# Layer 2 of a graph network: the edges' source product in float32r parts instead of float32

## The chip, the cores and the metric

The kernel runs on one core of one Trainium2 chip. The metric is the device time of one execution in microseconds (us). TensorE (PE) multiplies, ScalarE (ACT) and VectorE (DVE) read PSUM and SBUF, GpSimd (POOL) issues the indirect transfers, SyncE (SP) issues most of the others.

## The reference

There are 100,000 nodes with 128 features and 25,000 weighted edges, sorted by destination. Cut to what matters here:

```
h = relu(layernorm(x));  xn = bn0(h)
h1 = bn1(relu(gcn(xn) @ W1 ...))            # 128 -> 256
h2 = bn2(relu(agg(h1) @ Wrel2 + brel2 + h1 @ Wroot2))   # 256 -> 256
h3 = bn3(relu(agg(h2) @ Wrel3 + brel3 + h2 @ Wroot3))   # 256 -> 128
agg(h)[d] = sum over edges e into d of ew[e] * h[src[e]]
out = x + h3
```

`_bn` normalizes over the nodes and `_gcn_conv` is a weighted sum over the edges plus a self term, multiplied by W1.

## The kernel before

A node without an incoming edge needs only a dense product, and a destination of an edge needs more. So each layer has a dense part (98 tiles of 1024 nodes) and an edge part (49 chunks of 512 edges, 128 channels on the partitions, 512 edges along the free axis). Both are interleaved on every engine. The phases are: setup, norm (layernorm, and a fold of the first norm into W1), layers l1, l2, l3, and out.

Each engine has one in-order stream that `pipeline` writes out: in each turn the stages of `edge_layer`, then those of `dense_layer`, then `edges_ahead`; a chunk has a turn every second dense tile. A stage has a lag: the turn it runs in, counted in chunks. In layer 2 the lags are 1 for turning the gathered rows and making z (`l_turn`), 2 for the product of z (`l_src`), 3 for the weighted running sums (`l_sum`), 4 for their product with Wrel2 (`l_rel`), 5 for the destinations (`l_dst`). A PE stage waits on semaphores, and nothing behind it on the engine can pass it.

For the source end of an edge layer 2 makes its input again: `source_z` (VectorE, L1380 and L1383) multiplies the loaded rows `ed_hs` by the inverse degree and adds the turned gathered sum, which gives z; `source` (PE, L1298) multiplies z by W1 in two blocks of 128 columns; `source_relu` (ScalarE, L1466) evicts them; `affine` and `sums` go on from there. The other products of layer 2 are made in parts: a value is cast to float32r (top), the difference is kept (rest), and top*w_top + rest*w_top + top*w_rest are added up in PSUM. That is how the dense tiles (casts L1130, rests L1162, products L1103, evictions L1117), the sums (`sum_top` L1511, `sum_rest` L1421, `rel` L1314) and the destinations (L1534, L1524, `dst` L1338) are multiplied. The product of z is in plain float32.

The order of the edge stages on ScalarE and VectorE, as the kernel writes it (each with its lag), and the wait ahead of the product of z:

```
stages = [(l_rel, sum_top), (l_dst, table_out(0))] if n < 3 else []      # scalar
stages += [(l_dst, dst_relu)]
stages += [(l_dst, table_out(1))] if n == 2 else []
stages += [(l_src, source_relu), (l_src, affine)]

stages = [(l_rel, sum_rest)] if n == 2 else []                           # vector
stages += [(l_dst, statistics)]
stages += [(l_turn, source_z)] if n == 2 else []
stages += [(l_sum, sums)]

wait_use(pe, zz[j], i, 2)                                                # source
```

`table_out` (L1490) evicts the rows that `table` (PE, L1352) turned, `dst_relu` (L1502) evicts the destinations' product, and `statistics` (L1409) takes its moments. `turn` (PE, L1277) turns the gathered rows.

Of the kernel before, what the change touches and what calls it, by code (L numbers as in the profile page):

```python
# [23 lines left out]
FP = mybir.dt.float32  # L24
FR = mybir.dt.float32r
BF = mybir.dt.bfloat16
I32 = mybir.dt.int32
# [6 lines left out]
C = 128  # L34
# [72 lines left out]
def wait_use(eng, sem, i, per=1, upto=None, base=0):  # L107


    if isinstance(i, int) and i < 0:  # L110
        return
    eng.wait_ge(sem, i * per + (base + (per if upto is None else upto)))
# [83 lines left out]
def before(i, j, d, slots):  # L196

    return i - (d - j + slots - 1) // slots if d > j else i, (j - d) % slots
# [12 lines left out]
def build(nc, x, src, dst, ew, prm, out):  # L211
# [47 lines left out]
    with keep:  # L259
        def sb(name, shape, dt=FP):  # L260
            return keep.enter_context(nc.sbuf_tensor(name, shape, dt))
# [16 lines left out]
        out_c = sb("out_cols", [P, ET], I32)  # L278
        ew_c = sb("weight_cols", [P, ET])
        rounds_first = sb("rounds_first", [1, 2, EI], I32)  # L280
        rounds_norm = sb("rounds_norm", [1, 3, EI], I32)
        zeros_c = sb("zeros_c", [128, 1])
        no_edge_row = sb("no_edge_row", [P, 1, 1])
        neg_share = sb("neg_share_of_dst", [128, 1])
# [6 lines left out]
        def middle_sb(name, shape, dt=FP):  # L291
            return middle.enter_context(nc.sbuf_tensor(name, shape, dt))

        w1, wrel[2] = middle_sb("w1", [C, 1, H1]), middle_sb("wrel2", [C, 2, H1])
        wparts[2], wrel_parts = [[middle_sb(f"{name}_{part}", [C, 2, H1], FR) for part in ("top", "rest")] for name in ("wroot2", "wrel2")]
        dst_c, inv_c = middle_sb("dst_cols", [P, ET], I32), middle_sb("inv_deg_src_cols", [P, ET])
        front = middle.enter_context(ExitStack())
# [1 line left out]
        def front_sb(name, shape, dt=FP):  # L299
            return front.enter_context(nc.sbuf_tensor(name, shape, dt))  # L300

        wroot[2], wfold[1] = front_sb("wroot2", [C, 2, H1]), front_sb("w1_fold", [C, 1, H1])
        moments = front_sb("moments0", [C, TC])
        mval = front_sb("map_values", [P, ET, 2])
        src_c = front_sb("src_cols", [P, ET], I32)

# [863 lines left out]
        def edge_layer(ph, n, ps, slots):  # L1170
# [45 lines left out]
            for j in range(slots):  # L1216
                stood[j] += 16 * EG * uses(slots, j)
            if n == 2:
                inv = ph.sb("ed_inv", [C, slots, CW])
                s_top, s_rest, d_top = (ph.sb(f"ed_{x}", [C, kb, CW], FR) for x in ("sum_top", "sum_rest", "hd_top"))  # L1220
                d_rest = hd_in.bitcast(FR)
                s_tp, s_rs, d_tp, d_rs = (ph.slots(f"ed_{x}", slots) for x in ("sum_top", "sum_rest", "hd_top", "hd_rest"))
                ag = ph.sb("ed_rel", [C, slots, 2, CW])
                tb = ph.sb("ed_rows", [P, slots, EG, kb * C])
                tiles = tab[n][0:EP, :].rearrange("(t p g) c -> t p g c", p=P, g=EG)
                halves = kb
                hg = EG // halves
# [42 lines left out]
            def tensor(pe):  # L1270
# [9 lines left out]
                def source(i, j):  # L1280
                    i1, j1 = before(i, j, 1, slots)
                    if n == 2:
                        wait_use(pe, zz[j], i, 2)
                    else:
                        wait_use(pe, in_a[j], i, 16)
                        wait_use(pe, gat[j], i, 16 * EG, base=base[j])
                    for m in range(2):
                        wait_use(pe, rl_s[j1], i1, 2, m + 1)
                        o = ps[:, BS + m, 0:CW]
                        if n == 3:  # L1290

                            for g in range(EG):
                                ins = pe.matmul(ps[:, BS + m, g * P:(g + 1) * P], tg[:, j, g, m * C:(m + 1) * C], ident[0:P, 0:P],
                                                start=g == 0, stop=False, is_transpose=True, skip_group_check=True)
                            ins.then_inc(tu[j], 1)
                        for k in range(ks):
                            w = w1 if n == 2 else wfold[2]
                            ins = pe.matmul(o, w[:, k, m * C:(m + 1) * C], hsi[:, j, k, :],  # L1298
                                            start=n == 2 and k == 0, stop=k == ks - 1, skip_group_check=n == 3)
                        ins.then_inc(mm_s[j], 1)  # L1300

                def products(parts, top, rest, k, m):
# [70 lines left out]
            def vector(dve):  # L1373
                dve.memset(zero[:, :], 0.0).then_inc(z0, 1)
                dve.wait_ge(z0, 1)

                def source_z(i, j):

                    wait_use(dve, in_a[j], i, 32)
                    dve.tensor_tensor(hsi[:, j, 0, :], hsi[:, j, 0, :], inv[:, j, :], ALU.mult).then_inc(zz[j], 1)  # L1380
                    wait_use(dve, zz[j], i, 2, 1)
                    wait_use(dve, tu[j], i)
                    dve.tensor_tensor(hsi[:, j, 0, :], hsi[:, j, 0, :], ps[:, BG, 0:CW], ALU.add).then_inc(zz[j], 1)  # L1383

                def sums(i, j):
                    wait_use(dve, in_b[j], i, 16 * (4 - n))
                    if n == 3:
                        wait_use(dve, spr[j], i)
                    for k in range(kb):
                        wait_use(dve, aff[j], i, kb, k + 1)  # L1390
                        weight = cf[:, j, :] if n == 2 else ps[:, BW[j], 0:CW]
                        dve.tensor_tensor(xa[:, j, k, :], xa[:, j, k, :], weight, ALU.mult).then_inc(msg[j], 1)

                    if n == 2:
                        wait_use(dve, mm_r[j], i - 1, mb)
                    else:
                        wait_use(dve, mm_d[j], i - 1, mb)
                    i1, j1 = before(i, j, 1, slots)
                    wait_use(dve, scn[j1], i1, kb)
                    for k in range(kb):  # L1400
                        wait_use(dve, msg[j], i, kb, k + 1)
                        fresh = isinstance(i1, int) and i1 < 0
                        start = zero[:, 0:1] if fresh else se[:, j1, k, CW - 1:CW]
                        dve.tensor_tensor_scan(se[:, j, k, :], ss[:, j, :], xa[:, j, k, :], start, ALU.mult, ALU.add).then_inc(scn[j], 1)
                def statistics(i, j):
                    for m in range(mb):
                        wait_use(dve, rl_d[j], i, mb, m + 1)
                        dve.sem_inc(gate_d, 1)
                        dve.bn_stats(stats[:, m, NT * CH + i * slots + j, :], dst_out(i, j, m)).then_inc(st_d[j], 1)  # L1409

                def weights(i, j):
                    wait_use(dve, spr[j], i - 1)
                    dve.sem_inc(gate_w, 1)
                    dve.tensor_copy(cw[:, j, :], ew_c[:, bass.ds((i * slots + j) * EG, EG)]).then_inc(cwc[j], 1)

                def sum_rest(i, j):
                    i1, j1 = before(i, j, 1, slots)
                    wait_use(dve, mm_r[j1], i1, mb)
                    for k in range(kb):
                        wait_use(dve, s_tp[j], i, kb, k + 1)  # L1420
                        dve.tensor_tensor(s_rest[:, k, :], se[:, j, k, :], s_top[:, k, :].bitcast(FP), ALU.subtract).then_inc(s_rs[j], 1)  # L1421

                stages = [(l_rel, sum_rest)] if n == 2 else []
                stages += [(l_dst, statistics)]
                stages += [(0, weights)] if n == 3 else []
                stages += [(l_turn, source_z)] if n == 2 else []
                stages += [(l_sum, sums)]

                def end():
                    for j in range(slots):  # L1430
                        dve.wait_ge(st_d[j], mb * uses(slots, j))

                return slots, stages, end

            def scalar(act):
# [74 lines left out]
                        wait_use(act, scn[j], i, kb, k + 1)  # L1510
                        act.activation(s_top[:, k, :], se[:, j, k, :], ACT.Copy).then_inc(s_tp[j], 1)  # L1511

                stages = [(l_rel, sum_top), (l_dst, table_out(0))] if n < 3 else []
                stages += [(l_dst, dst_relu)]
                stages += [(l_dst, table_out(1))] if n == 2 else []
                stages += [(l_src, source_relu), (l_src, affine)]
# [25 lines left out]
        def fold(ph, n, blocks, groups, weight, folded, b_in, b_out, ps=None):  # L1542
# [25 lines left out]
            def vector(dve):  # L1568
                done = [0]

                def link(ins):
                    done[0] += 1
                    ins.then_inc(s, 1)
                    dve.wait_ge(s, done[0])
# [44 lines left out]
                if n in (1, 2):  # L1619
                    for (w_top, w_rest), w in ((wparts[n + 1], folded), (wrel_parts, wrel[2]))[:3 - n]:  # L1620
                        link(dve.tensor_copy(w_top[:, :, :], w[:, :, :]))
                        link(dve.tensor_tensor(w_rest[:, :, :], w[:, :, :], w_top[:, :, :].bitcast(FP), ALU.subtract))
                for m in range(b_in.shape[1]):
                    dve.wait_ge(pd, m + 1)
                    link(dve.tensor_tensor(b_out[:, m:m + 1], b_in[:, m:m + 1], ps[:, m, 0:1], ALU.add))
# [183 lines left out]
```

## Time and profile before

| | |
|---|---|
| median of 3 runs | 3447.38 us (3444.28 to 3447.8) |
| the profiled execution | 3449.69 us, its span 3447.9 us |
| busy in the span | PE 2844.8, DVE 2603.7, ACT 2310.8, POOL 1310.1 us |
| layer 2 | from about 1119 to 2205 us of the span |

The span runs from the first to the last instruction. Matmuls overlap, so the start of one to the start of the next tells more than the duration of one; their ends are modelled. A float32 matmul has two records. "f32" in the type of a matmul stands for float32 and float32r alike. In brackets is the idle time of the engine just before an instruction and what ended it. In a table of windows the columns are: the stretch, its length, busy time (and instructions) of PE, of the weight loads PEld, of DVE, ACT and POOL, then the granted clock of TensorE as a share of 2.4 GHz, the busy share of the DMA engines, and GB/s.

### The profile page before, as it was taken

Reading aid. Unit: us, or ns where it says so; the run is one execution under the profiler, and the core shown is the slowest. Engines: PE = TensorE matmul, PEld = TensorE weight load, DVE = VectorE, ACT = ScalarE, POOL = GpSimd, SP = SyncE. Lnnn points to the kernel's source line nnn. Section 1 sums busy time; section 2 is a strip of 40 time slices with the busy share of each in tenths; the row PEclk is TensorE's granted clock in tenths of the full one; section 3 lists DMA queues with packets and bytes.
Section 4 is the critical chain, followed back from the end, with each engine's and each line's share of the span. In section 5 each row is a group of like instructions: output and inputs, shape, how many; then the busy total and the mean of one; then the engine's idle time right before and its main releaser. Section 6 shows DMA issues by size and latency. Waiting matters only on the chain. (4 is left out here: it accounts for less than half of the span.)

```text
span 3447.9 us, 51737 instructions
## 1 busy us (share of the span) xinstructions
PE 2844.8 (83%) x12445; PEld 1955.9 (57%) x12445; DVE 2603.7 (76%) x5601; ACT 2310.8 (67%) x4070; POOL 1310.1 (38%) x1196
## 2 busy tenths in 40 slices
PE   3666499999997899999999999699999999554542
PEld 2666355555554677777777777555555555443432
DVE  6999388888888788888888888678888888533332
ACT  4999377777775688888888887466666667333331
POOL 1657656556551421111211110132222221266576
PEclk9999799999998999999999999899999999655555
DMA  5999499999996799999999999589999998799997
GB/s 193 344 344 328 133 333 345 339 342 340 337 339 253 271 345 344 346 347 344 344 347 346 344 348 329 185 295 339 340 339 341 340 339 316 288 365 363 381 357 227
DMA packets 335138, 1106.81 MB, mean 321 GB/s; under 512 B 54569, under 2 KB 102210, under 8 KB 285906
## 3 DMA queue, kind: packets, MB, share of 16 engines
q1 hardware_dynamic: 211964, 905.05, 71.8%
q0 software_dynamic: 62656, 77.70, 10.0%
q10 hardware_dynamic: 60438, 123.18, 9.9%
q8 instruction: 27, 0.44, 0.1%
q14 instruction: 53, 0.43, 0.0%
HBM read 599.13 MB, written 498.21 MB: 318 GB/s over the span
## 5 line engine op out<-in xcount | busy, mean ns | idle before, releaser
L1265 POOL DMA_INDIRECT l_ed_gathered<-agg_rows,pos_cols x392 | 399.8, 1020 | 1419.1 <-PE l_ps L1277 699.8
L1162 DVE TENSOR_TENSOR dense_tiles<-dense_tiles,l_dn_top 128x512 fp32r<-128x512 f32 x784 | 501.7, 688 | 235.1 <-ACT l_dn_top L1130 235.1
L1103 PE MATMUL l_ps<-l_dn_top,wroot_top 128*128 128x512 f32 x1176 | 502.6, 427 | 73.2 <-ACT l_dn_ho L1117 43.3
L1130 ACT ACTIVATE l_dn_top<-dense_tiles 128x512 fp32r<-128x512 f32 x784 | 447.8, 623 | 32.1 <-issue 31.7
L1103 PE MATMUL l_ps<-l_dn_top,wroot_rest 128*128 128x512 f32 x1176 | 468.3, 398 | 0.0
L1103 PE MATMUL l_ps<-dense_tiles,wroot_top 128*128 128x512 f32 x1176 | 463.0, 394 | 0.0
L745 PE MATMUL l_ps<-l_dn_columns,w_fold 128*128 128x512 f32 x784 | 382.0, 610 | 31.0 <-ACT l_dn_ho L780 31.0
L1117 ACT ACTIVATE l_dn_ho<-l_ps,bias_fold 128x512 f32<-128x512 f32 x392 | 263.4, 685 | 160.0 <-PE l_ps L1103 159.5
L1733 PE MATMUL out_ps<-ident,dense_tiles 128*128 128x128 f32 x784 | 185.6, 415 | 208.6 <-ACT dense_tiles L1720 208.6
L1103 PEld LDWEIGHTS l_ps<-l_dn_top,wroot_top 128*128 128x128 f32 x1176 | 222.6, 189 | 183.3 <-ACT l_dn_ho L1117 64.2
L1749 DVE TENSOR_TENSOR out_od_ot<-out_ps,x_tiles 128x512 f32<-128x512 f32 x196 | 134.7, 691 | 246.9 <-PE out_ps L1733 242.8
L627 ACT ACTIVATE norm_ln_ho<-norm_ln_x,norm_ln_nbias,norm_ln_rstd 128x128 f32<-128x128 f32 x784 | 301.7, 480 | 0.0
L639 PE MATMUL norm_ln_ps<-norm_ln_ho 128*128 128x130 f32 x1568 | 202.8, 282 | 116.7 <-ACT norm_ln_ho L627 116.7
L780 ACT ACTIVATE l_dn_ho<-l_ps,bias_fold 128x512 f32<-128x512 f32 x392 | 260.3, 694 | 47.7 <-PE l_ps L745 40.7
L1720 ACT ACTIVATE dense_tiles<-dense_tiles,bn_shift,bn_scale 128x1024 f32<-128x1024 f32 x98 | 121.3, 1239 | 252.0 <-DMA dense_tiles<-h_dense 242.4
L1733 PEld LDWEIGHTS out_ps<-ident,dense_tiles 128*128 128x128 f32 x784 | 148.8, 217 | 245.2 <-ACT dense_tiles L1720 161.8
L863 POOL DMA_INDIRECT l_ed_dst_rows<-h_rows,dst_cols x196 | 208.8, 1065 | 167.7 <-PE l_ps L945 117.9
L639 PEld LDWEIGHTS norm_ln_ps<-norm_ln_ho 128*128 128x128 f32 x1568 | 184.2, 191 | 135.5 <-ACT norm_ln_ho L627 135.5
L1103 PEld LDWEIGHTS l_ps<-dense_tiles,wroot_top 128*128 128x128 f32 x1176 | 223.5, 190 | 58.1 <-issue 12.0
L669 POOL DMA_INDIRECT h_rows<-map_values,out_cols x196 | 189.5, 967 | 169.6 <-issue 154.1
L1103 PEld LDWEIGHTS l_ps<-l_dn_top,wroot_rest 128*128 128x128 f32 x1176 | 222.6, 189 | 54.5
L745 PEld LDWEIGHTS l_ps<-l_dn_columns,w_fold 128*128 128x128 f32 x784 | 134.1, 191 | 208.4 <-ACT l_dn_ho L780 140.9
(247 smaller groups left out, 6245.9 us busy)
## 6 DMA issues: line engine op xcount, KB each, us to landing
h_dense<-l_dn_ho SPq DMA_DIRECT2D x188, 1024.0 KB, 10.8
dense_tiles<-h_dense SPq DMA_DIRECT2D x188, 1024.0 KB, 8.6
l_dn_rows<-h_rows SPq DMA_DIRECT2D x98, 520.0 KB, 6.9
h_rows<-norm_ln_ho SPq DMA_DIRECT2D x97, 520.0 KB, 4.3
h_dst<-l_ed_ho SPq DMA_DIRECT2D x98, 512.0 KB, 6.3
l_ed_hd<-h_dst ACTq DMA_DIRECT2D x98, 512.0 KB
norm_ln_x<-in_x SPq DMA_DIRECT2D x97, 512.0 KB, 5.4
x_tiles<-in_x SPq DMA_DIRECT2D x97, 512.0 KB, 15.3
```

The source lines that it names most:

```text
L627: ins = act.activation(ho[:, j, g, 0:C], xt[:, j, g, :], ACT.Relu, bias=nb[:, j, g:g + 1], scale=rs[:, j, g:g + 1])
L639: ins = pe.matmul(ps[:, 0, 0:TC], ho[0:rows, j, g, 0:C], ho[0:rows, j, g, :], start=first and g == 0, stop=final and g == G - 1, skip_grou ...
L669: pool.indirect_dma_start(h0[:, :], bass.IndirectOffsetOnAxis(ap=out_c[0:rows, t:t + 1], axis=0), mval[0:rows, t, :], None, element_offset ...
L745: pe.matmul(ps[:, 2 + u % 2, 0:CW], wfold[1][:, 0, m * C:(m + 1) * C], hc[:, j % 2, c * CW:(c + 1) * CW], start=True, stop=True).then_inc( ...
L780: act.activation(ho[:, j, m, c * CW:(c + 1) * CW], ps[:, 2 + u % 2, 0:CW], ACT.Relu, bias=bfold[1][:, m:m + 1]).then_inc(rl[j], 1)
L863: pool.indirect_dma_start(to[:, j, g, :], None, h0[0:N, :], bass.IndirectOffsetOnAxis(ap=idx[:, t:t + 1], axis=0)).then_inc(gat[j], 16)
L1103: ins = pe.matmul(o, a, b, start=t == 0, stop=t == len(terms) - 1)
L1117: act.activation(ho[:, j, m, c * CW:(c + 1) * CW], ps[:, u % 2, 0:CW], ACT.Relu, bias=bf[:, m:m + 1]).then_inc(rl[j], 1)
L1130: act.activation(top[:, j % 2, k, cc], hi[:, j, k, cc], ACT.Copy).then_inc(tp[j], 1)
L1162: dve.tensor_tensor(rest[:, j, k, cc], hi[:, j, k, cc], top[:, j % 2, k, cc].bitcast(FP), ALU.subtract).then_inc(spl[j], 1)
L1265: pool.indirect_dma_start(tg[:, j, g, :], None, tab[n - 1][:, :], bass.IndirectOffsetOnAxis(ap=pos_c[:, t:t + 1], axis=0)).then_inc(gat[j] ...
L1733: ins = pe.transpose(ps[0:P, bank0 + (j % 2) * banks + b, g * C:(g + 1) * C], hi[:, j, e:e + P], ident[:, :])
```

## The change

The product of z with W1 in layer 2 is made like the others, in float32r parts. W1's parts are made once, in the fold at the end of the norm phase. ScalarE casts z to `ed_z_top` in the new stage `z_cast`, VectorE makes `ed_z_rest` in the new stage `z_remainder`, both with the lag of the product, and the product waits for the remainder. Each part has one buffer. `w1` and `rounds_norm` move to memory that is given back after layer 1.

```diff
             if n == 2:
+                z_top, z_rest = ph.sb("ed_z_top", [C, CW], FR), ph.sb("ed_z_rest", [C, CW], FR)
+                z_tp, z_rs = ph.slots("ed_z_top", slots), ph.slots("ed_z_rest", slots)
...
                     if n == 2:
-                        wait_use(pe, zz[j], i, 2)
+                        wait_use(pe, z_rs[j], i)
...
-                        for k in range(ks):
-                            w = w1 if n == 2 else wfold[2]
-                            ins = pe.matmul(o, w[:, k, m * C:(m + 1) * C], hsi[:, j, k, :],
-                                            start=n == 2 and k == 0, stop=k == ks - 1, skip_group_check=n == 3)
+                        mc = slice(m * C, (m + 1) * C)
+                        if n == 2:
+                            terms = [(w1_top[:, mc], z_top[:, :]), (w1_top[:, mc], z_rest[:, :]), (w1_rest[:, mc], z_top[:, :])]
+                        else:
+                            terms = [(wfold[2][:, k, mc], hsi[:, j, k, :]) for k in range(ks)]
+                        for t, (a, b) in enumerate(terms):
+                            ins = pe.matmul(o, a, b, start=n == 2 and t == 0, stop=t == len(terms) - 1, skip_group_check=n == 3)
                         ins.then_inc(mm_s[j], 1)
...
+                def z_remainder(i, j):
+                    wait_use(dve, z_tp[j], i)
+                    dve.tensor_tensor(z_rest[:, :], hsi[:, j, 0, :], z_top[:, :].bitcast(FP), ALU.subtract).then_inc(z_rs[j], 1)
...
-                stages += [(l_turn, source_z)] if n == 2 else []
+                stages += [(l_src, z_remainder), (l_turn, source_z)] if n == 2 else []
...
-                stages = [(l_rel, sum_top), (l_dst, table_out(0))] if n < 3 else []
+                def z_cast(i, j):
+                    i1, j1 = before(i, j, 1, slots)
+                    wait_use(act, mm_s[j1], i1, 2)
+                    wait_use(act, zz[j], i, 2)
+                    act.activation(z_top[:, :], hsi[:, j, 0, :], ACT.Copy).then_inc(z_tp[j], 1)
+
+                stages = [(l_src, z_cast), (l_rel, sum_top), (l_dst, table_out(0))] if n < 3 else []
...
+                if n == 0:
+                    link(dve.tensor_copy(w1_top[:, :], w1[:, 0, :]))
+                    link(dve.tensor_tensor(w1_rest[:, :], w1[:, 0, :], w1_top[:, :].bitcast(FP), ALU.subtract))
```

On VectorE the edge turn of a steady period of layer 2 reads so before the change, from the remainders of the sums over the statistics of the destinations and z to the running sums:

```order
L1421 TENSOR_TENSOR l_ed_sum_rest<-l_ed_sum,l_ed_sum_top 128x512 x2
L1409 BN_STATS bn_stats_all<-l_ed_ho 128x6 x2
L1380 TENSOR_TENSOR l_ed_hs<-l_ed_hs,l_ed_inv 128x512
L1383 TENSOR_TENSOR l_ed_hs<-l_ed_hs,l_ps 128x512
L1392 TENSOR_TENSOR l_ed_xa<-l_ed_xa,l_ed_coef 128x512 x2
L1404 SCALAR_TENSOR_TENSOR l_ed_sum<-l_ed_same,l_ed_sum,l_ed_xa 128x512 x2
```

And so with the change, in which the line numbers are higher by up to 19:

```order
L1431 TENSOR_TENSOR l_ed_sum_rest<-l_ed_sum,l_ed_sum_top 128x512 x2
L1419 BN_STATS bn_stats_all<-l_ed_ho 128x6 x2
L1393 TENSOR_TENSOR l_ed_z_rest<-l_ed_hs,l_ed_z_top 128x512
L1386 TENSOR_TENSOR l_ed_hs<-l_ed_hs,l_ed_inv 128x512
L1389 TENSOR_TENSOR l_ed_hs<-l_ed_hs,l_ps 128x512
L1402 TENSOR_TENSOR l_ed_xa<-l_ed_xa,l_ed_coef 128x512 x2
L1414 SCALAR_TENSOR_TENSOR l_ed_sum<-l_ed_same,l_ed_sum,l_ed_xa 128x512 x2
```

The remainder of z stands behind the statistics of the destinations and ahead of the next chunk's z; nothing else moved.

On ScalarE the same place with the change is the following, from the last casts of a dense tile to the evictions of the product of z:

```order
L1131 ACTIVATE l_dn_top<-dense_tiles 128x512 x2
L112 ISA x2
L1527 ACTIVATE l_ed_z_top<-l_ed_hs 128x512
L112 ISA
L112 REGISTER_ALU
L1521 ACTIVATE l_ed_sum_top<-l_ed_sum 128x512 x2
L112 REGISTER_ALU
L1500 ACTIVATE l_ed_rows<-l_ps 128x512
L112 ISA
L1512 ACTIVATE l_ed_ho<-l_ps,bias_fold 128x512 x2
```

The row of `l_ed_z_top` is new and stands ahead of the casts of the sums; the two evictions `l_ed_ho`, for which the statistics on VectorE wait, come three stages behind it.

## Rows read from the trace of the kernel before

**Rows 1.** Windows of the steady part of layer 2 (columns as told above).

```profile
1160.00:2100.00 940.00, 898.06 (x3913) 676.54 (x3912) 810.33 (x1227) 760.28 (x1312) 181.02 (x176) 1.00 0.98 344
```

**Rows 2.** Waits in 1160 to 2100 us: us in total, times, longest.

```profile
PE l_ps L1103 <- ACT l_dn_ho L1117: 39.8, 43, 2.0
```

**Rows 3.** Timeline of PE in one period: start, us, instruction.

```profile
1610.45 0.66 PE L1352 MATMUL l_ps<-ident,l_ed_rel 128*128 128x128 f32 x4
1610.94 0.60 PE L1277 MATMUL l_ps<-ident,l_ed_gathered 128*128 128x128 f32 x4
1611.38 1.88 PE L1298 MATMUL l_ps<-l_ed_hs,w 128*128 128x512 f32 x4
...
1613.34 0.39 PE L1314 MATMUL l_ps<-l_ed_sum_rest,wrel_top 128*128 128x512 f32 x1
...
1615.67 0.40 PE L1314 MATMUL l_ps<-l_ed_sum_top,wrel_rest 128*128 128x512 f32 x1
...
1632.84 1.88 PE L1298 MATMUL l_ps<-l_ed_hs,w 128*128 128x512 f32 x4
```

**Rows 4.** Timeline of ACT in the same period.

```profile
1608.77 1.15 ACT L1511 ACTIVATE l_ed_sum_top<-l_ed_sum 128x512 fp32r<-128x512 f32 x2
1609.81 0.59 ACT L1490 ACTIVATE l_ed_rows<-l_ps 128x512 f32<-128x512 f32 x1
1610.29 0.69 ACT L1502 ACTIVATE l_ed_ho<-l_ps,bias_fold 128x512 f32<-128x512 f32 x1
...
1610.86 0.69 ACT L1502 ACTIVATE l_ed_ho<-l_ps,bias_fold 128x512 f32<-128x512 f32 x1
...
1612.44 0.69 ACT L1466 ACTIVATE l_ed_ho_src<-l_ps,bias 128x512 f32<-128x512 f32 x1 [0.30 <-PE l_ps L1298]
```

**Rows 5.** Timeline of DVE in the same period.

```profile
1609.60 1.29 DVE L1421 TENSOR_TENSOR l_ed_sum_rest<-l_ed_sum,l_ed_sum_top 128x512 fp32r<-128x512 f32 x2
1611.24 1.29 DVE L1409 BATCH_NORM_STATS2 bn_stats_all<-l_ed_ho 128x512 f32 x2 [0.35 <-ACT l_ed_ho L1502]
1612.44 0.68 DVE L1380 TENSOR_TENSOR l_ed_hs<-l_ed_hs,l_ed_inv 128x512 f32<-128x512 f32 x1
1613.15 0.69 DVE L1383 TENSOR_TENSOR l_ed_hs<-l_ed_hs,l_ps 128x512 f32<-128x512 f32 x1
...
1621.52 1.29 DVE L1162 TENSOR_TENSOR dense_tiles<-dense_tiles,l_dn_top 128x512 fp32r<-128x512 f32 x2 [1.73 <-ACT l_dn_top L1130]
```

**Rows 6.** Timelines at two waits of PE that end, with what ended one.

```profile
1164.88 1.28 DVE L1421 TENSOR_TENSOR l_ed_sum_rest<-l_ed_sum,l_ed_sum_top 128x512 fp32r<-128x512 f32 x2
...
1165.62 0.50 PE L1314 MATMUL l_ps<-l_ed_sum_top,wrel_top 128*128 128x512 f32 x1 [2.10 <-DVE l_ed_sum_rest L1421]
...
1603.84 0.50 PE L1103 MATMUL l_ps<-l_dn_top,wroot_top 128*128 128x512 f32 x1 [0.87 <-ACT l_dn_ho L1117]
1604.18 0.39 PE L1103 MATMUL l_ps<-dense_tiles,wroot_top 128*128 128x512 f32 x1
```

**Rows 7.** Timelines of PE and DVE at the first chunk of layer 2.

```profile
1143.98 1.88 PE L1298 MATMUL l_ps<-l_ed_hs,w 128*128 128x512 f32 x4
...
1145.21 1.29 DVE L1162 TENSOR_TENSOR dense_tiles<-dense_tiles,l_dn_top 128x512 fp32r<-128x512 f32 x2 [0.32 <-ACT l_dn_top L1130]
1146.42 0.69 DVE L1380 TENSOR_TENSOR l_ed_hs<-l_ed_hs,l_ed_inv 128x512 f32<-128x512 f32 x1
```

**Rows 8.** Timeline at the end of the norm phase: last fold step, a scatter.

```profile
361.41 0.17 DVE L1627 TENSOR_SCALAR quiet<-bias_fold 128x2 f32<-128x2 f32 x1
...
364.45 0.91 POOL L669 DMA_INDIRECT h_rows<-map_values,out_cols  x1 [0.30 <-issue]
```

**Rows 9.** A wait of PE, and windows with the granted clock behind two waits.

```profile
1189.39 0.50 PE L1103 MATMUL l_ps<-l_dn_top,wroot_top 128*128 128x512 f32 x1 [1.60 <-ACT l_dn_ho L1117]
...
1167.10:1170.20 3.10, 3.10 (x9) 2.33 (x9) 2.06 (x4) 0.79 (x2) 2.38 (x3) 0.50 1.04 412
...
1189.40:1192.80 3.40, 3.40 (x18) 2.82 (x18) 0.86 (x2) 2.24 (x5) 0.00 (x0) 1.00 1.01 385
```

More of the change, by code:

```diff
@@ L280, in build @@
         rounds_first = sb("rounds_first", [1, 2, EI], I32)
-        rounds_norm = sb("rounds_norm", [1, 3, EI], I32)
         zeros_c = sb("zeros_c", [128, 1])
@@ L292, in middle_sb @@
             return middle.enter_context(nc.sbuf_tensor(name, shape, dt))
-        w1, wrel[2] = middle_sb("w1", [C, 1, H1]), middle_sb("wrel2", [C, 2, H1])
+        wrel[2] = middle_sb("wrel2", [C, 2, H1])
+        w1_top, w1_rest = middle_sb("w1_top", [C, H1], FR), middle_sb("w1_rest", [C, H1], FR)
         wparts[2], wrel_parts = [[middle_sb(f"{name}_{part}", [C, 2, H1], FR) for part in ("top", "rest")] for name in ("wroot2", "wrel2")]
@@ L302, in build @@
         wroot[2], wfold[1] = front_sb("wroot2", [C, 2, H1]), front_sb("w1_fold", [C, 1, H1])
-        moments = front_sb("moments0", [C, TC])
+        w1, moments = front_sb("w1", [C, 1, H1]), front_sb("moments0", [C, TC])
+        rounds_norm = front_sb("rounds_norm", [1, 3, EI], I32)
         mval = front_sb("map_values", [P, ET, 2])
```

## The prediction

> **What bounds the kernel now.** I read the stages first (the windows by stretch), then the waits of layer 2, then one period of its loop instruction by instruction, because the change only touches the edge chunks of layer 2 and a small fold ahead of layer 1. In the steady part of layer 2 [rows 1] TensorE is busy 898.06 of 940 us at full clock, VectorE 810.33, ScalarE 760.28, and the DMA engines 98%. One period (one chunk of 512 edges and two dense tiles) is 21.45 us: the product of z starts at 1611.38 and again at 1632.84 [rows 3]. The DMA share looks like a second bound, but the waits of this stretch name no dense tile or store; what TensorE waits for is ScalarE's eviction of the dense tile's products, 39.8 us in 43 times [rows 2], 0.93 us each. So the loop runs at TensorE's pace, plus one short stop per period. What holds up TensorE once per period holds up all of layer 2. The other engines have room: VectorE idles 1.73 us before the dense rests [rows 5].
>
> What sets the place of each engine near the product of z is the order in which each one takes its stages. TensorE does the last products for the destinations, turns the second half of the table (1610.45), turns the gathered rows (1610.94) and goes straight into the product of z at 1611.38 [rows 3]. ScalarE at that moment is not ahead but behind: from 1608.77 it casts the sums' top, evicts table rows (1609.81), evicts the two destination products (1610.29 and 1610.86), back to back, and only then waits for the product of z [rows 4]. VectorE follows ScalarE: the statistics of the destinations start at 1611.24 and the next instruction at 1612.44 [rows 5]. Today the product of z doesn't care, since its z was finished a period ago.
>
> **The change part by part.** (a) *The product itself.* The two float32 products are four matmul records, and from the first to the second record of the product behind them it takes 1613.34 - 1611.38 = 1.96 us. Eleven float32r matmuls from 1613.34 to 1615.67 are 10 steps, 0.233 us each [rows 3]. So the old product takes 1.96 - 0.233 = 1.73 us, the new one 6 x 0.233 = 1.40: TensorE gains 0.33 us a chunk, 16 us over 49 chunks. If nothing waited this would be the result.
>
> (b) *The cast on ScalarE.* The new cast stands ahead of the casts of the sums. Two such casts take 1.04 us of the queue (1608.77 to 1609.81 [rows 4]), so one takes 0.52. Its inputs are long ready (z was added up in the previous period, the product before has been done for a period). But ScalarE is back to back there, so everything behind it moves by 0.52: the table eviction that the second turn of the table waits for, and the eviction of the destination products, the last of which starts at 1610.86 + 0.52 = 1611.38.
>
> (c) *The remainder on VectorE.* It stands behind the destination statistics and ahead of the next chunk's z. The statistics wait for those evictions (they start 0.26 us after the first one's end, 1610.29 + 0.69 [rows 4, 5]), so they move by the same 0.52 and VectorE is free at 1612.44 + 0.52 = 1612.96. A subtraction of this size takes 0.69 (the row of the z addition, 0.69, and two remainders in 1.29 [rows 5]): the remainder ends at 1613.65. TensorE restarts 0.05 behind such a subtraction: the first of the pair at 1164.88 ends at about 1165.57, TensorE goes on at 1165.62 [rows 6]. So the product of z can start at 1613.70 instead of 1611.38: **TensorE stands 2.32 us**. The wait is at the head of the product and holds the queue: behind it are the twelve products of the sums, then both dense tiles, and ScalarE's source evictions wait for it too. None of them can pass.
>
> (d) *Restart.* After a wait the first matmul takes 0.34 to the next one's start (1603.84 to 1604.18 [rows 6]) instead of 0.233: +0.11.
>
> Per chunk: 2.32 + 0.11 - 0.33 = **+2.10 us**. Does something take it back? The stop of 0.87 us before a dense product at 1603.84 [rows 6] comes from ScalarE's order behind TensorE's own evictions, so it moves along with TensorE and stays. ScalarE has 0.52 and VectorE 0.69 more work in a period that grows by 2.1; neither becomes the bound. The gathers wait for the turn, which moves only 0.5. Transfers get more time.
>
> How many chunks: 46 of 49 have the destination stages in the loop (they start 3 chunks later than the products of z): 46 x 2.10 = 96.6 us. For the first three, VectorE stands in the dense rests instead: the product is at 1143.98, the last rests start at 1145.21 and the next instruction, whose place the remainder takes, at 1146.42, so the remainder ends at 1147.11, TensorE goes on at 1147.16, a stop of 3.18; with (a) and (d) +2.96 each, 9 us [rows 7].
>
> (e) *The fold of the first norm* gets two more VectorE instructions on half of 128x512, each below 0.69 [rows 5], say 0.6 together. I take it at nothing: VectorE's last step of the fold is at 361.41 while GpSimd still issues scatters at 364.45 [rows 8], and the stage ends for all engines together. Uncovered it would cost 0.6. The moved buffers cost nothing in time; I find no stage that uses another amount of memory traffic.
>
> (f) *The clock.* Layer 2 has had some longer stops of TensorE. After the one of 2.10 us at 1165.62 [rows 6] the granted clock was 0.50 (1.2 GHz) from 1167.1 to 1170.2, with 9 matmuls in 3.1 us; after the one of 1.60 at 1189.39 it stayed at 1.00 (2.4 GHz) with 18 in 3.4 us [rows 9]. At 0.233 a matmul, 3.1 us would hold 13.3, so such a stretch loses 4.3 x 0.233 = 1.0 us by the count and up to half of 3.1, 1.55, by the level of the clock. I take 1.5. The new stop of 2.32 is cut in two by the turns: 0.52 before the second turn of the table, 1.8 before the product. That lies between the two cases seen. I choose one fall in nine chunks, 5 x 1.5 = 7.5 us; the ends are none and all 49 (73 us).
>
> The Trainium skill ("TensorE: Matmul & The Clock Gate", section "HAM oscillation — how this bites in real kernels") says that a loop whose waits let the clock fall pays for it again in each iteration. By that rule, if it applies here, the time is the upper end, 3626 us; the trace has both cases, a fall after 2.10 and none after 1.60, so it bears the rule out only for the longer stops.
>
> **Sum.** 96.6 + 9 + 7.5 = 113 us on the profiled execution's 3449.7 us (span 3447.9) gives 3562.8; the runs' median 3447.4 is 2.3 lower, so **3560 us**.
>
> **The rivals.**
> 1. *The clock falls often.* The same stop, but the half clock comes in every second chunk or more: 3447.4 + 105.6 + 25 to 49 times 1.5 = 3590 to 3626. For it: a fall after 2.10. Against it: the turns break the stop, and none fell after 1.60.
> 2. *The stop is shorter.* If ScalarE's cast finds room (0.52 drops out), a chunk costs 1.58: 46 x 1.58 + 9 = 82, 3529. Against it: ScalarE shows no idle time from 1608.77 to the eviction at 1610.86, and the table's turn waits for it already.
> 3. *Faster: the remainder is ready in time.* Then only (a) is left, 3447.4 - 16 = 3431. It decides at one point: the subtraction would have to end by 1611.33. VectorE's statistics alone, ahead of it, don't end before 1612.44 today. It needs VectorE to run the remainder ahead of the statistics, which the order doesn't do. The same with a stop of just 0.2 a chunk is no change.
> 4. *DMA takes over.* The share of 98% at a period of 21.45 speaks for a bound near today's time; with a longer period there is less traffic per time, so it can only hide a gain, not add. It would make rival 3 end at no change.
>
> **How the numbers follow.** Forecast (2.0 to 2.2 per chunk, clock falls in at most one chunk in three) 0.64; rival 1 0.16; rival 2 0.13; rivals 3 and 4 0.03 together, of it 0.02 faster and 0.01 the same; anything slower than 3626 or between 0.2% and 80 us slower 0.04. A difference of 0.2% (7 us) is about what a measurement of this kernel can tell from no change. Slower by over 0.2%: 0.97. The range goes from the shorter stop (3529, taken as 3530) up into the cases where the clock falls every second chunk: 3600.
>
> **What the profile would show.** TensorE waits on VectorE's remainder once a chunk, about 1.65 to 1.8 us by the profile's way of ending matmuls, some 80 us in total; the period is 23.5 us; the six matmuls step by 0.233; the remainder starts right at the end of the destination statistics; the destination evictions lie 0.52 later against the dense ones; layers 1, 3 and the output stage are unchanged. The granted clock of layer 2 tells how often it fell. The prediction is wrong if the remainder comes before the statistics, if the stop of 0.87 us at the dense products shrinks as the new one grows, or if the clock falls in most chunks.

## The result, and the profile after

The changed kernel takes 3565.71 us (median of 5 runs, 3560.26 to 3569.77), the kernel before 3446.91 us (5 runs, 3444.28 to 3447.8): ratio 1.0342, 95% interval [1.0328, 1.0356], 3.4% slower. Three executions lie far off whatever the kernel (of the experiments below e6 has one of 3624.17 us at a granted clock of 0.80, e7 one of 6755.06, and the kernel before beside e9 and e10 one of 5905.29); they are in the medians, which they hardly move, and in no ratio. The profiled execution took 3560.67 us. From the head of its page:

```profile
span 3558.9 us, 52062 instructions
...
PE 2855.4 (80%) x12543; PEld 1983.1 (56%) x12543; DVE 2635.8 (74%) x5652; ACT 2333.8 (66%) x4119; POOL 1322.9 (37%) x1196
```

The span grew by 111.0 us, but TensorE's busy time by only 10.6: the loss is waiting. The first gathered rows of layer 2 are turned at 1133.67 us of the span (1133.36 before), and an equal stretch of layer 3 before and after reads alike; first before, from 2225 us, then after, from 2338 us:

```profile
2225.00:2960.00 735.00, 711.70 (x2622) 429.55 (x2621) 585.56 (x914) 490.46 (x832) 191.04 (x188) 0.98 0.91 319
```

```profile
2338.00:3073.00 735.00, 710.66 (x2624) 429.19 (x2622) 586.56 (x916) 490.79 (x833) 191.03 (x189) 0.99 0.91 320
```

So it is in layer 2: from its first turn of gathered rows to the first one of layer 3 the profiled execution takes 112.7 us more, and 2.1 less from there to the end. Its window and its waits after (us in total, times, longest), against [rows 1, 2]:

```profile
1160.00:2200.00 1040.00, 907.02 (x3997) 700.01 (x3998) 839.65 (x1267) 779.61 (x1351) 193.62 (x179) 0.99 0.92 310
```

```profile
PE l_ps L1305 <- DVE l_ed_z_rest L1393: 81.5, 46, 4.6
...
PE l_ps L1104 <- ACT l_dn_ho L1118: 35.9, 40, 1.6
```

TensorE now waits for the remainder of z once a chunk; the old stop at the dense tiles is still there, 0.87 us in the steady part as before. DMA went from 98% busy at 344 GB/s to 92% at 310. One period of the loop on TensorE, against [rows 3]:

```profile
1616.31 0.66 PE L1358 MATMUL l_ps<-ident,l_ed_rel 128*128 128x128 f32 x4 [0.42 <-ACT l_ed_rows L1500]
1616.80 0.60 PE L1280 MATMUL l_ps<-ident,l_ed_gathered 128*128 128x128 f32 x4
1619.12 0.49 PE L1305 MATMUL l_ps<-l_ed_z_top,w_top 128*128 128x512 f32 x1 [1.71 <-DVE l_ed_z_rest L1393]
1619.45 0.40 PE L1305 MATMUL l_ps<-l_ed_z_rest,w_top 128*128 128x512 f32 x1
...
1620.62 0.40 PE L1320 MATMUL l_ps<-l_ed_sum_top,wrel_top 128*128 128x512 f32 x1
...
1640.44 0.60 PE L1280 MATMUL l_ps<-ident,l_ed_gathered 128*128 128x128 f32 x4
```

The stop is in two pieces, 0.42 before the table's second turn and 1.71 before the product. The product takes 1.50 us with its restart, and the period is 1640.44 - 1616.80 = 23.64 us. ScalarE and VectorE in the same period, against [rows 4] and [rows 5]:

```profile
1614.10 0.63 ACT L1527 ACTIVATE l_ed_z_top<-l_ed_hs 128x512 fp32r<-128x512 f32 x1
1614.63 1.15 ACT L1521 ACTIVATE l_ed_sum_top<-l_ed_sum 128x512 fp32r<-128x512 f32 x2
1615.67 0.58 ACT L1500 ACTIVATE l_ed_rows<-l_ps 128x512 f32<-128x512 f32 x1
...
1616.15 0.68 ACT L1512 ACTIVATE l_ed_ho<-l_ps,bias_fold 128x512 f32<-128x512 f32 x1
...
1616.72 0.69 ACT L1512 ACTIVATE l_ed_ho<-l_ps,bias_fold 128x512 f32<-128x512 f32 x1
...
1620.11 1.40 ACT L1476 ACTIVATE l_ed_ho_src<-l_ps,bias 128x512 f32<-128x512 f32 x2 [2.22 <-PE l_ps L1305]
```

```profile
1617.09 1.29 DVE L1419 BATCH_NORM_STATS2 bn_stats_all<-l_ed_ho 128x512 f32 x2 [0.51 <-ACT l_ed_ho L1512]
1618.30 0.68 DVE L1393 TENSOR_TENSOR l_ed_z_rest<-l_ed_hs,l_ed_z_top 128x512 fp32r<-128x512 f32 x1
...
1629.04 1.29 DVE L1163 TENSOR_TENSOR dense_tiles<-dense_tiles,l_dn_top 128x512 fp32r<-128x512 f32 x2 [2.81 <-ACT l_dn_top L1131]
```

The reader sees the chain whole: the cast at 1614.10 holds ScalarE's evictions up by 0.53, the statistics on VectorE wait for them, the remainder comes at 1618.30 right behind the statistics, and TensorE starts 0.14 us behind its end at 1618.98. VectorE is not short of time: it is idle for 2.81 us ahead of the dense rests, 1.73 before. The remainder is late by its place, not by VectorE's load. The first chunk has the other form, with the dense rests ahead of the remainder, against [rows 7]:

```profile
1145.58 1.29 DVE L1163 TENSOR_TENSOR dense_tiles<-dense_tiles,l_dn_top 128x512 fp32r<-128x512 f32 x2 [0.32 <-ACT l_dn_top L1131]
1146.79 0.69 DVE L1393 TENSOR_TENSOR l_ed_z_rest<-l_ed_hs,l_ed_z_top 128x512 fp32r<-128x512 f32 x1
...
1147.54 0.79 PE L1305 MATMUL l_ps<-l_ed_z_top,w_top 128*128 128x512 f32 x1 [3.02 <-DVE l_ed_z_rest L1393]
```

From one turn of gathered rows to the next, the 48 intervals of the layer give nearly the whole account of the profiled execution. Before, the last 40 are 21.45 to 21.48 us. After, 34 of them are 23.44 to 23.66 and six 25.00 to 25.15, together 95.1 us more. The first eight intervals add 13.2 us. Of the six long ones, this is one; matmul starts first, then the window right behind the stop, and the same place in a period of 23.64:

```profile
1952.84 0.79 PE L1305 MATMUL l_ps<-l_ed_z_top,w_top 128*128 128x512 f32 x1 [1.71 <-DVE l_ed_z_rest L1393]
1953.42 0.63 PE L1305 MATMUL l_ps<-l_ed_z_rest,w_top 128*128 128x512 f32 x1
1953.85 0.63 PE L1305 MATMUL l_ps<-l_ed_z_top,w_rest 128*128 128x512 f32 x1
```

```profile
1952.90:1955.90 3.00, 3.00 (x7) 2.41 (x8) 2.96 (x5) 0.79 (x2) 2.10 (x3) 0.50 0.91 373
...
1642.80:1645.80 3.00, 3.00 (x13) 2.45 (x14) 2.88 (x5) 1.56 (x3) 2.08 (x4) 1.00 0.96 381
```

The granted clock is 0.50 (1.2 GHz) while the whole product of z runs, its matmuls step by 0.43 instead of 0.233, and the interval is 1.4 us longer. It fell so at the product behind the last turn too, which is in none of the 48 intervals:

```profile
2215.24 0.74 PE L1305 MATMUL l_ps<-l_ed_z_top,w_top 128*128 128x512 f32 x1 [1.51 <-DVE l_ed_z_rest L1393]
```

```profile
2215.40:2218.60 3.20, 3.20 (x8) 2.52 (x9) 3.17 (x5) 1.14 (x2) 0.00 (x0) 0.50 0.80 334
```

### The profile page after: what moved, and what is told of

The parts are those of the page before. It is cut to its first block and busy times, and to the rows that moved or that the text cites. A ratio compares the mean times of both kernels' runs of the same rounds, so it can differ in the third digit from the quotient of the medians.

```text
span 3558.9 us, 52062 instructions
## 1 busy us (share of the span) xinstructions
PE 2855.4 (80%) x12543; PEld 1983.1 (56%) x12543; DVE 2635.8 (74%) x5652; ACT 2333.8 (66%) x4119; POOL 1322.9 (37%) x1196
## 5 line engine op out<-in xcount | busy, mean ns | idle before, releaser
L1268 POOL DMA_INDIRECT l_ed_gathered<-agg_rows,pos_cols x392 | 409.9, 1046 | 1519.5 <-PE l_ps L1280 794.1
L1739 ACT ACTIVATE dense_tiles<-dense_tiles,bn_shift,bn_scale 128x1024 f32<-128x1024 f32 x98 | 121.3, 1239 | 251.8 <-DMA dense_tiles<-h_dense 241.8
```

The lines of the kernel that those rows point to most:

```text
L1268: pool.indirect_dma_start(tg[:, j, g, :], None, tab[n - 1][:, :], bass.IndirectOffsetOnAxis(ap=pos_c[:, t:t + 1], axis=0)).then_inc(gat[j] ...
```

## The experiments

The theory: TensorE pays what stands ahead of the remainder, on VectorE and (through the statistics) on ScalarE, and each piece adds up. The rivals are in the expectations. All times are medians; ratios are to the kernel before on the same chip (3447.27 us beside e1 to e4, 3449.34 beside e5 to e8, 3589.01 beside e9 and e10). Line numbers in some kernels are a few higher than in the changed one.

**The remainder first (e1).** Edit to the changed kernel:

```diff
-                stages = [(l_rel, sum_rest)] if n == 2 else []
+                stages = [(l_src, z_remainder), (l_rel, sum_rest)] if n == 2 else []
...
-                stages += [(l_src, z_remainder), (l_turn, source_z)] if n == 2 else []
+                stages += [(l_turn, source_z)] if n == 2 else []
```

> The changed kernel with one move: on VectorE the remainder of z stands ahead of the remainders of the sums, not behind the destination statistics. The cast stays where it is. Theory A (the stop is made by what stands ahead of the remainder on VectorE): the remainder ends before TensorE has turned the gathered rows; what is left is the cast's 0.52 us a chunk ahead of the table eviction, less the 0.33 of the faster product, so +0.2 for 46 chunks, and still about 3 us for each of the first three chunks, where the dense rests stand ahead: about 3465 us, no clock falls. Theory B (the stop comes with the parts as such, wherever they are made): it stays near 3560.

Measured: 3462.05 us, ratio 1.0042 [1.0027, 1.0057]. VectorE, then TensorE, in one period:

```profile
1618.28 0.68 DVE L1393 TENSOR_TENSOR l_ed_z_rest<-l_ed_hs,l_ed_z_top 128x512 fp32r<-128x512 f32 x1
1618.88 1.29 DVE L1431 TENSOR_TENSOR l_ed_sum_rest<-l_ed_sum,l_ed_sum_top 128x512 fp32r<-128x512 f32 x2
1620.44 1.29 DVE L1419 BATCH_NORM_STATS2 bn_stats_all<-l_ed_ho 128x512 f32 x2 [0.27 <-ACT l_ed_ho L1512]
```

```profile
1619.66 0.66 PE L1358 MATMUL l_ps<-ident,l_ed_rel 128*128 128x128 f32 x4 [0.42 <-ACT l_ed_rows L1500]
1620.15 0.60 PE L1280 MATMUL l_ps<-ident,l_ed_gathered 128*128 128x128 f32 x4
1620.51 0.48 PE L1305 MATMUL l_ps<-l_ed_z_top,w_top 128*128 128x512 f32 x1
```

The product follows the turn without a stop, and only the 0.42 before the table's turn is left; it goes where the cast moves (e2, e3), so it is the cast's. The steady period is 21.67 us, +0.21 to before. TensorE stops for the remainder in three chunks only, 9.1 us together, the first three. This one move takes back 104 of 119 us.

**The cast moved (e2).** Edit to the changed kernel:

```diff
-                stages = [(l_src, z_cast), (l_rel, sum_top), (l_dst, table_out(0))] if n < 3 else []
+                stages = [(l_rel, sum_top), (l_dst, table_out(0))] if n < 3 else []
...
-                stages += [(l_rel, rel_out)] if n == 2 else []
+                stages += [(l_rel, rel_out), (l_turn, z_cast)] if n == 2 else []
```

> The changed kernel with the other move alone: the cast of z stands at the end of ScalarE's edge stages, one chunk earlier, where ScalarE waits for dense products; the remainder stays behind the statistics. Theory A (cast and remainder add up in one chain): the stop shrinks by the cast's 0.52 us, from +2.18 to +1.66 a chunk: 76 + 9 us and a few falls of the clock, about 3537 us. Rival (the cast's place doesn't matter, since the statistics wait for something else): no change, 3565.

Measured: 3553.62 us (3544.94 to 3563.64), ratio 1.0298 [1.0275, 1.0321], 17 above the forecast. The period at full clock is 23.10 us, 0.53 below the changed kernel's, as expected. But every second one is 24.66, with a stop of the same length ahead of it:

```profile
1670.92 0.52 PE L1305 MATMUL l_ps<-l_ed_z_top,w_top 128*128 128x512 f32 x1 [1.71 <-DVE l_ed_z_rest L1393]
```

```profile
1671.30:1674.60 3.30, 3.30 (x9) 2.61 (x8) 3.27 (x6) 1.38 (x2) 2.69 (x3) 0.50 0.92 378
```

The window right behind the restart is at clock 0.50 for 3.3 us. So the term of the cast is right, and by the medians the clock takes back half of it. How often the clock falls changes from execution to execution: the profiled one, with every second period long from about 1380 us on, took 3563.64 us, another 3561.72 (mean granted clock 0.905 and 0.906), and the other two 3544.94 and 3545.52 (0.911 and 0.912).

**Both moved a chunk ahead (e3).** The cast as above, and on VectorE:

```diff
-                stages += [(l_src, z_remainder), (l_turn, source_z)] if n == 2 else []
+                stages += [(l_turn, source_z)] if n == 2 else []
                 stages += [(l_sum, sums)]
+                stages += [(l_turn, z_remainder)] if n == 2 else []
```

> Both moves: the cast at the end of ScalarE's edge stages and the remainder at the end of VectorE's, one chunk ahead of the product. Theory A: TensorE never waits for the parts and gains 0.33 us on each of 49 chunks, the period goes from 21.45 to 21.13 us: about 3431 us, faster than both kernels. Rival (the DMA engines, 98% busy in layer 2, bound it at today's period): 3447, with waits on transfers in layer 2.

Measured: 3438.13 us (3432.3 to 3443.47), ratio 0.9965 [0.9952, 0.9979]: 0.35% faster than before, 7 us above the forecast. TensorE, with the next period's turn, then VectorE and ScalarE:

```profile
1614.49 0.60 PE L1280 MATMUL l_ps<-ident,l_ed_gathered 128*128 128x128 f32 x4
1614.85 0.47 PE L1305 MATMUL l_ps<-l_ed_z_top,w_top 128*128 128x512 f32 x1
...
1635.64 0.60 PE L1280 MATMUL l_ps<-ident,l_ed_gathered 128*128 128x128 f32 x4
```

```profile
1620.90 0.66 DVE L1393 TENSOR_TENSOR l_ed_z_rest<-l_ed_hs,l_ed_z_top 128x512 fp32r<-128x512 f32 x1
...
1620.06 0.63 ACT L1528 ACTIVATE l_ed_z_top<-l_ed_hs 128x512 fp32r<-128x512 f32 x1
```

The remainder is ready 14 us before its product of the next period. The period is 21.15 us, 0.32 below before, so the product's gain is real, and DMA at 98% was not the bound at 21.45. Over 40 chunks that would be 13 us (12 measured, since the first of them is 21.87); the start of the layer gives 4.6 of it back in the profiled execution, in its first four intervals. There the remainder stands behind the messages, and these behind a transfer (e10 below loses most of the 4.6 without it); VectorE, then TensorE, at the third chunk:

```profile
1164.37 1.29 DVE L1402 TENSOR_TENSOR l_ed_xa<-l_ed_xa,l_ed_coef 128x512 f32<-128x512 f32 x2 [3.59 <-DMA l_ed_coef<-row_weight]
...
1167.95 0.70 DVE L1393 TENSOR_TENSOR l_ed_z_rest<-l_ed_hs,l_ed_z_top 128x512 fp32r<-128x512 f32 x1
...
1168.70 0.80 PE L1305 MATMUL l_ps<-l_ed_z_top,w_top 128*128 128x512 f32 x1 [2.85 <-DVE l_ed_z_rest L1393]
```

**The product in float32 (e4).** In the changed kernel `w1` stays, its parts go to the memory that is given back, and:

```diff
-                            terms = [(w1_top[:, mc], z_top[:, :]), (w1_top[:, mc], z_rest[:, :]), (w1_rest[:, mc], z_top[:, :])]
+                            terms = [(w1[:, 0, mc], hsi[:, j, 0, :])]
```

> The changed kernel, with cast, remainder and wait where they are, but the product itself in float32 as before the change (the parts are made and not used). Theory A: the period grows by the 0.33 us that float32r saves, 16 us over 49 chunks, about 3582 us (more or fewer clock falls aside). Rival (the float32r product saves nothing behind a stop, since its evictions or the restart hide it): 3566.

Measured: 3574.7 us (3572.55 to 3577.59), ratio 1.037 [1.0354, 1.0386]. The period is 23.95 us, 0.32 above the changed kernel's, as the theory says. The time is 7 below the forecast since the clock did not fall once from 1260 to 2200 us in the profiled execution, where the changed kernel lost six times 1.4 us, although the stops are as long:

```profile
1260.00:2200.00 940.00, 821.24 (x3532) 609.95 (x3532) 752.42 (x1139) 704.01 (x1219) 170.04 (x156) 1.00 0.93 309
```

```profile
PE l_ps L1306 <- DVE l_ed_z_rest L1394: 67.9, 40, 1.7
```

**The stop filled (e5).** To the kernel with the cast moved:

```diff
                     if n == 2:
+                        wait_use(pe, rl_s[j1], i1, 2)
+                        for _ in range(5):
+                            pe.matmul(ps[:, BS, 0:CW], w1_top[:, 0:C], wrel_parts[0].rearrange("c k h -> c (k h)"), start=True, stop=True)
                         wait_use(pe, z_rs[j], i)
```

> e2_cast_idle with five more float32r matmuls (1.17 us) on TensorE ahead of the wait for the remainder, into the bank that the product then starts anew; they are work for nothing. In the profile of e2 a period was 23.10 us, but 24.66 in every second chunk, right behind a stretch of half clock. Theory C (the half clock comes of TensorE's idle time at the stop): with the stop filled all periods are 23.10 us or little more, 21 stretches of 1.55 us go: 3554 - 33 = about 3521 us up to 3532. Rival (the clock falls for another reason, load or heat, or the filler is paid in full): 3554, or 3554 + 49 x 1.17 = 3611.

Measured: 3531.34 us, ratio 1.0242 [1.0226, 1.0257]. TensorE does 220 matmuls more in this window (its product of z is L1308) and the kernel is 22 us faster than e2 by the medians, and its slowest run is 13 below e2's fastest. Nearly all steady periods are 23.09 to 23.26 us:

```profile
1200.00:2200.00 1000.00, 938.19 (x4190) 724.01 (x4191) 822.93 (x1250) 772.43 (x1341) 182.92 (x168) 1.00 0.95 320
```

```profile
PE l_ps L1308 <- DVE l_ed_z_rest L1396: 22.3, 44, 0.5
```

What is left, 82 us above before (3449.34 on that chip), is the stop with its restart less the gain of the product: 23.10 - 21.46 = 1.64 a chunk.

**Both moved, nearer to z (e6, e10).** The cast between `source_relu` and `affine`, the remainder between `source_z` and `sums`, both with lag `l_turn`:

```diff
+                stages += [(l_src, source_relu)] + ([(l_turn, z_cast)] if n == 2 else []) + [(l_src, affine)]
...
+                stages += [(l_turn, source_z), (l_turn, z_remainder)] if n == 2 else []
```

> Both moves as in e3_both_early, but nearer to z: the cast between the source evictions and the affine on ScalarE, the remainder right behind the addition that makes z and ahead of the messages and scans on VectorE. In e3 the steady period was 21.14 us but the first chunks of layer 2 lost time, since the remainder stood behind a wait of the messages for a transfer. Theory A: the same 21.14 us and a start like before the change: about 3431 us, 0.4% below before. Rival (VectorE's wait for the cast, about 0.8 us, or the later affine delays a dense tile): period above 21.14, 3440 or more.

Measured: 3438.51 us, ratio 0.9969 [0.9957, 0.9981], no better than e3. The profiled execution is the one of 3624.17 us, so no period is told from it. On another chip the same kernel again:

> e6_both_near_z once more, for an undisturbed profile. Theory A: period 21.14 us, and no stop at the product of z in the first chunks of layer 2: 3431 to 3438 us. Rival: the place nearer to z costs on the first chunks what e3 paid there (4.5 us), or TensorE stops somewhere else once a chunk.

Measured: 3576.85 us against 3589.01 before on that chip, ratio 0.9973 [0.996, 0.9986]. That chip takes more time in the norm phase (223 GB/s against 301 in the window from 40 to 560 us), so only the ratio counts. The steady period is 21.15 us in 31 of 40, the other nine are about 21.8, and TensorE doesn't stop for the remainder at all. Still the first four intervals take 50.2 us against 46.5 before. So what e3 lost there, 4.6 us, did not hang on the stop of 2.85 at the product alone: with that stop gone, 3.7 are still lost. The trace shows where: TensorE stops for 1.02 us at two dense products (0.70 before), for 1.21 and 0.97 at two others where it did not, and for 3.59 ahead of the products of the sums (2.10 in [rows 6], but 3.24 in e7, whose layer 2 is the one of before). Why the two dense products have to wait is left open.

**Memory and fold alone (e7).** The kernel before with the moved buffers and the two fold instructions.

> The kernel before with only the moved buffers and the two more instructions of the fold that make W1's parts (not used). Theory A: 3447, nothing measurable. Rival (the placement in memory or the fold costs what is not seen in layer 2): above 3449.

Measured: 3448.73 us, ratio 1.0001 [0.9991, 1.001]: nothing.

**One instruction more ahead (e8).**

```diff
                     wait_use(dve, z_tp[j], i)
...
+                    dve.bn_stats(z_spare[:, :], hsi[:, j, 0, :]).then_inc(z_once, 1)
```

> The changed kernel with one more instruction of 0.69 us (0.6 us of the queue: statistics of z into a spare tile) on VectorE right ahead of the remainder. Theory A (every instruction ahead of the remainder is paid on TensorE): period 23.63 + 0.6 = 24.24 us, 29 us over 49 chunks, 3595 us with few clock falls, up to 3650 where the longer stop makes them frequent. Rival (VectorE has room for it): 3566.

Measured: 3641.88 us, ratio 1.0561 [1.0545, 1.0577]. The periods are 25.5 and 25.7 in turn, with a stretch of half clock in each:

```profile
1200.00:2200.00 1000.00, 855.35 (x3599) 663.62 (x3598) 777.59 (x1178) 704.84 (x1217) 159.94 (x161) 0.94 0.87 291
```

```profile
PE l_ps L1306 <- DVE l_ed_z_rest L1397: 91.1, 40, 2.3
```

The stop grew from 1.71 to 2.3 us by the instruction's own 0.6 on VectorE, which accounts for 49 x 0.6 = 29 us (a period of 24.24, reckoned: none here is free of half clock). The other 47 of the 76 us over the changed kernel are put down to the clock: the periods are 1.3 to 1.5 us above 24.24.

**The two single moves together (e9).**

> The two single moves together: the cast as in e2_cast_idle, the remainder as in e1_rest_first (ahead of the remainders of the sums, in the product's own turn). Theory A (the terms add up): no stop in the steady part, period 21.14 us (-0.32 a chunk, as e3 had), but the 3 us in each of the first three chunks stay, since there the dense rests stand ahead of the remainder: 3447 - 15 + 9 = 3441 us. Rival (the two moves together don't do more than e1, which has a period of 21.67): 3462.

Measured on the chip of 3589.01: 3579.84 us, ratio 0.9984 [0.9971, 0.9997]; the forecast's 3441 to 3447 is 0.9983. 26 of the last 40 periods are 21.14 or close to it, 14 are 21.8 to 21.9 for a reason that is left open, and the three stops of the first chunks are there, 9.1 us together.

## Why the prediction was right

Predicted 3560 us with a range of 3530 to 3600, measured 3565.71.

- *What bounds:* that TensorE set the pace of layer 2 at 21.46 and DMA did not is shown by the period of 21.15 in e3. How much further it could fall is not shown: from 1260 to 2100 us of e3 the DMA engines are 100% busy at 349 GB/s.
- *(a) the product:* predicted -0.33 us a chunk; e3 shows -0.32, e4 +0.32.
- *(b) the cast:* predicted 0.52; e2's period is 0.53 below the changed one, e1's rest is +0.21 for 0.52 - 0.33 = 0.19.
- *(c) and (d) the stop:* predicted +2.10 a chunk with (a), measured +2.18 in a period without a clock fall. The 0.08 more are the handover: TensorE started 0.14 behind the end of the remainder, not 0.05.
- *How many chunks:* this was off in the parts. The three intervals with the long stop add 3.3 us on average where 2.96 was predicted. The stops are 3.02, 3.02 and 4.57 us where 3.18 was said for each: in the third chunk the remainders of the sums stand ahead of the remainder of z as well, which the prediction did not count. Part of that was there before, as the stop of 2.10 at the products of the sums [rows 6], and this one is gone. After, VectorE, then TensorE:

```profile
1172.09 1.29 DVE L1431 TENSOR_TENSOR l_ed_sum_rest<-l_ed_sum,l_ed_sum_top 128x512 fp32r<-128x512 f32 x2 [0.26 <-ACT l_ed_sum_top L1521]
```

```profile
1174.04 0.63 PE L1305 MATMUL l_ps<-l_ed_z_top,w_top 128*128 128x512 f32 x1 [4.57 <-DVE l_ed_z_rest L1393]
```

  The four intervals behind them add 3.2 together where 4 x 2.10 = 8.4 was predicted. There the old stops of TensorE went away as the new ones came. Before, it stopped at dense products for 1.60 [rows 9], 1.32 and 2.04 us up to 1260 us; after, one stop of 1.62 at the dense products is left in that stretch, beside the new pair of 0.42 and 1.51 at each product of z. Before, then after:

```profile
1220.49 0.50 PE L1103 MATMUL l_ps<-l_dn_top,wroot_top 128*128 128x512 f32 x1 [1.32 <-ACT l_dn_ho L1117]
...
1237.55 0.50 PE L1103 MATMUL l_ps<-l_dn_top,wroot_top 128*128 128x512 f32 x1 [2.04 <-ACT l_dn_ho L1117]
```

```profile
1226.00 0.51 PE L1305 MATMUL l_ps<-l_ed_z_top,w_top 128*128 128x512 f32 x1 [1.51 <-DVE l_ed_z_rest L1393]
...
1251.96 0.50 PE L1104 MATMUL l_ps<-l_dn_top,wroot_top 128*128 128x512 f32 x1 [1.62 <-ACT l_dn_ho L1118]
```

  The prediction had said that a stop at the dense products is not absorbed. For the steady part that holds (about 0.87 a chunk in both kernels), for these chunks it does not. The sum hides it: 13.2 for the first eight intervals, 95.1 for the last forty and 2.7 outside them (0.3 ahead, 4.5 from the last turn to layer 3, 2.1 less behind) make 111.0, where 113 were predicted.
- *(e) memory and fold:* nothing, shown by e7.
- *(f) the clock:* five falls at 1.5 us were chosen. In the profiled execution six at 1.4 lie in the last forty intervals, three behind the stops of the first three chunks and one at the product behind the last turn, ten in all; in the same loop the kernel before has two, at about 1167 [rows 9] and 1239 us. The size is shown; that the count in the steady part came so near was luck, since e2 and e4 have stops of the same length and falls in every second period and in none. Of the rivals, the clock is the one with substance: it took 17 us over the forecast for the kernel with the cast moved and 47 with one instruction more ahead. The rule of the Trainium skill ("TensorE: Matmul & The Clock Gate", section "HAM oscillation — how this bites in real kernels") that such a loop pays in each iteration came out in that last kernel alone; in the changed kernel six periods of 40 paid.
- The five runs spread over 9.5 us, against 3.5 before. Only one was profiled; that the number of falls makes the spread fits, and e2's two pairs of runs speak for it, but it is not shown for this kernel, whose mean granted clock is 0.912 or 0.913 in all five.

## What to carry to other kernels

Where the bounding engine waits for a new stage, the stage costs what stands ahead of it in its own engine's order, here +2.18 us a chunk, and not its own 0.69: the same cast, subtraction and product cost 3.4% in one place and give 0.3% in another. Before placing an instruction that the bounding engine waits for, find in the timeline which instruction it will follow and what that one waits for. If the input is ready a period earlier, as z was, make the parts then.

## What the runs showed of the hardware that was not expected

- TensorE's granted clock went to 0.50 (1.2 GHz) behind stops as short as 1.51 us (at 2215.24 us in the changed kernel, with a stop of 0.42 shortly ahead of it) and 1.71 us (e2), for the 3.2 and 3.3 us of the windows shown, and each such stretch in the steady part cost 1.4 to 1.56 us. At the same stop of 1.7 us it fell in every second period of 23.10 us, in 6 of 40 of 23.64, and in none of 23.95: the length of the stop alone does not decide it.
- Useless matmuls in a stop can pay: 1.17 us of them (5 x 0.233) in each chunk made the kernel with the moved cast 22 us faster.
- A float32 matmul of 128x512 has two records of 0.43 us each, and three float32r ones at 0.233 us step faster: for a pair of blocks six of these are 1.40 us against 1.73, 0.33 less, and the period shows 0.32.
